# Attention stage of a four-layer kernel: the gates' running products are broadcast by DMA instead of by TensorE, the state is carried by a diagonal matmul, the LayerNorm sums are taken by ScalarE

## What is computed

```
q = elu(0.25 x Wq')+1 ; k = elu(x Wk')+1 ; v = x Wv' ; gate = sigmoid(x Wg' + bg)     (one gate per head and token)
S_t = gate_t * S_{t-1} + k_t (outer) v_t ;  y_t = q_t S_t                              (16x16 state per head and sequence)
x1 = layernorm(x + y Wo')
```

## Time and profile before

| | |
|---|---|
| median of three runs | 1479.38 us |
| the profiled execution, its own time | 1477.29 us |
| its span in the profile | 1475.2 us |
| mean granted TensorE clock | 0.972 of full speed |
| attention stage (to the first instruction of the routing stage) | 0 to 326.5 us |
| busy over the span | PE 92%, DVE 56%, ACT 36%, POOL 21% |

### The profile page before, as it was taken

The page is one execution under the profiler, slowest core; times in us unless marked ns, Lnnn a source line. Parts: engine busy times, 40 slices in busy tenths (PEclk is TensorE's granted clock), DMA queues, the critical chain, the costliest instruction groups (busy, mean ns, idle before and its releaser), DMA issues. The chain is left out here.

```text
span 1475.2 us, 21868 instructions
## 1 busy us (share of the span) xinstructions
PE 1355.2 (92%) x7418; PEld 863.6 (59%) x7419; DVE 829.0 (56%) x1676; ACT 536.6 (36%) x1104; POOL 303.8 (21%) x357
## 2 busy tenths in 40 slices
PE   7898888889999899999999996969999999899996
PEld 4566666565545566666666664435666554477774
DVE  5999999976543122222222221447778855676764
ACT  5445555432101122222222221133444532467675
POOL 2123333221663000000000001613220000134444
PEclk9999999999999999999999998889999999999998
DMA  5544554629221111111111112303110000000001
GB/s 188 194 151 174 177 170 165 208 75 361 86 86 43 29 43 46 46 43 46 46 43 46 46 43 71 100 17 112 31 29 1 1 1 11 1 1 15 29 15 58
DMA packets 68226, 112.39 MB, mean 76 GB/s; under 512 B 9008, under 2 KB 53936, under 8 KB 64048
## 3 DMA queue, kind: packets, MB, share of 16 engines
q1 hardware_dynamic: 61584, 94.49, 19.2%
q0 software_dynamic: 6144, 16.79, 3.6%
q10 hardware_dynamic: 416, 0.03, 0.0%
HBM read 79.70 MB, written 31.59 MB: 75 GB/s over the span
## 5 line engine op out<-in xcount | busy, mean ns | idle before, releaser
L1681 POOL DMA_INDIRECT m_got<-outs,slot x64 | 61.2, 956 | 574.7 <-POOLq L2063 458.1
L1086 DVE TENSOR_TENSOR ro_h<-ro_bB,ro_sl 128x512 f32<-128x512 f32 x71 | 49.1, 691 | 222.2 <-PE ro_bB L1035 222.2
L515 DVE TENSOR_TENSOR_SCAN a_dcy<-a_gbc,a_ident 128x2048 f32<-128x2048 f32 x32 | 144.7, 4522 | 11.4 <-DMA a_gbc<-gd 7.5
L2035 POOL TENSOR_TENSOR q_hr<-q_hf,q_hr 128x512 fp32r<-128x512 f32 x64 | 83.4, 1314 | 287.6 <-ACT q_hr L1876 287.6
L1030 PE MATMUL ro_bA<-Win,ro_xT 128*128 x284 | 136.4, 603 | 0.7 <-ACT ro_xT L1057 0.5
L1042 PE MATMUL ro_bO<-Wout,ro_hT 128*128 x568 | 134.3, 379 | 0.9 <-DVE ro_hT L1079 0.9
L1042 PEld LDWEIGHTS ro_bO<-Wout,ro_hT 128*128 128x128 f32 x568 | 107.8, 190 | 45.6 <-issue 34.6
L1035 PE MATMUL ro_bB<-Wsw,ro_xT 128*128 x284 | 134.4, 596 | 0.0
L1079 DVE COPY ro_hT<-ro_bH 128x512 f32<-128x512 f32 x71 | 49.1, 691 | 101.3 <-PE ro_bH L1015 101.3
L1066 ACT ACTIVATE ro_yo<-ro_bO 128x256 f32<-128x256 f32 x71 | 27.2, 383 | 204.9 <-PE ro_bO L1042 204.9
L1035 PEld LDWEIGHTS ro_bB<-Wsw,ro_xT 128*128 128x128 f32 x284 | 54.5, 192 | 69.0 <-issue 69.0
(11 more groups left out here) (271 smaller groups left out, 2534.4 us busy)
## 6 DMA issues: line engine op xcount, KB each, us to landing
a_gbc<-gd SPq DMA_DIRECT2D x32, 1024.0 KB, 4.7
rows<-a_zero SPq DMA_DIRECT2D x8, 1152.0 KB, 10.4
ro_xg<-rows SPq DMA_DIRECT2D x71, 128.0 KB, 2.0
outs<-ro_yo SPq DMA_DIRECT2D x71, 128.0 KB, 1.7
a_xt<-in_xTt SPq DMA_DIRECT2D x8, 512.0 KB, 3.8
X<-in_x SPq DMA_DIRECT2D x8, 512.0 KB, 5.7
Win<-in_w_in SPq DMA_DIRECT2D x8, 512.0 KB, 10.7
Wsw<-in_w_sw SPq DMA_DIRECT2D x8, 512.0 KB, 10.6
```

What stands on the lines that cost most here:

```text
L515: v.tensor_tensor_scan(dcy[:, :], gbc[j % 2][:, :], ident16[:, :], 0.0, ALU.mult, ALU.add).then_inc(d_done, 1)
L1681: pool.indirect_dma_start(out=got[q % 2][k][:, t, :], out_offset=None, in_=mem["outs"], in_offset=bass.IndirectOffsetOnAxis(ap=slot[:, k, ...
L2035: pool.tensor_tensor(hr[:, 1, f % 4, :], hf[f % 2][:, :], hr[:, 0, f % 4, :], ALU.subtract).then_inc(hl_done, 1)
```

## The change

The running products ET go to DRAM (tensor `ed`) with four DMAs a chunk, and come back by two DMAs a tile, each row repeated for the 16 channels of its head, into ebc (four buffers). decayed_q reads ebc in SBUF. The state update is a matmul of a diagonal matrix dg (made by ScalarE from the last column of ebc) with the old state, added in PSUM to k times v, and VectorE only masks the sum into St. The LayerNorm sums come from two ScalarE instructions with accumulated outputs, one step later (tile n-2), and normalize, turn_x and router come one step later too (one more step in the loop). TensorE and ScalarE take project(n+5) early in the step, except in every fourth (Q % 4 == 0). spread stands behind phi(4T+10). ET of chunk 0 is not computed. The diff, shortened:

```diff
@@ sync
-                sp.dma_start(rep[:, :, :, :], io["rep"]).then_inc(cst_in, 16)
+                sp.dma_start(eye32[:, :], io["eye32"]).then_inc(cst_in, 16)
+                def decays_out(T):
+                    sp.wait_ge(e_done, T)
+                    for b in range(B):
+                        sp.dma_start(mem["ed"][T, b], ET[T % 2][32 * b:32 * b + H, :]).then_inc(ed_out, 16)
+                def decays_in(j):
+                    T, b = divmod(j, 4)
+                    if b == 0:
+                        sp.wait_ge(ed_out, 64 * T)
+                    if j >= 8:
+                        sp.wait_ge(qe_done, j - 7)
+                        sp.wait_ge(dg_done, 2 * min(j - 7, KEPT - 4))
+                    for g in range(G):
+                        sp.dma_start(ebc[j % 4][:, g, :], mem["ed"][T, b, 8 * g:8 * g + 8, :].unsqueeze(1).to_broadcast([8, DH, P])).then_inc(eb_in[j % 4], 16)
                     if n % 4 == 0 and n // 4 + 1 < NC:
                         gates_out(n // 4 + 1)
+                        decays_out(n // 4 + 1)
                     if n + 2 < NT:
                         gates_in(n + 2)
+                    if 4 <= n + 2 < NT:
+                        decays_in(n + 2)
@@ tensor
-                def decays(j):
...
                 def update(j):
-                    if j >= 3:
-                        pe.wait_ge(dec_done, j - 2)
...
-                                           start=True, stop=True)
+                                           start=(g == 0), stop=(j < 4), skip_group_check=True)
+                    if j >= 4:
+                        pe.wait_ge(dg_done, 2 * (j - 3))
+                        pe.wait_ge(st_done, j - 3)
+                        for g in range(G):
+                            for r in range(4):
+                                mm = pe.matmul(bK[32 * r:32 * r + 32, 32 * g:32 * g + 32], dg[j % 2][32 * r:32 * r + 32, g, :],
+                                               St[32 * r:32 * r + 32, j % 4, g, :], start=False, stop=True, skip_group_check=True)
...
-                    if tile(n - 3):
-                        decays(n + 1)
+                    if Q < NT and Q % 4 > 0:
+                        project(Q)
                     if tile(n - 1):
                         project_out(n - 1)
...
-                    if Q < NT:
+                    if Q < NT and Q % 4 == 0:
                         project(Q)
                     if tile(n + 1):
                         values(n + 1)
-                    if carries(n - 6):
-                        turn_x(n - 6)
+                    if carries(n - 7):
+                        turn_x(n - 7)
@@ scalar
+                def decay_matrix(j):
+                    act.wait_ge(eb_in[j % 4], 32 * (j // 4))
+                    if j >= 6:
+                        act.wait_ge(u_ready, j - 1)
+                    for g in range(G):
+                        act.activation(dg[j % 2][:, g, :], eye32[:, :], ACT.Copy, scale=ebc[j % 4][:, g, P - 1:P]).then_inc(dg_done, 1)
+                def moments(j):
...
+                    act.activation(scrap[:, :], X[:, j, :], ACT.Copy, scale=-1.0 / D, accum_out=mv[T % 2][:, b, 0:1]).then_inc(bn_done, 1)
+                    act.wait_ge(bn_done, j + 1)
+                    act.activation(scrap[:, :], X[:, j, :], ACT.Square, bias=mv[T % 2][:, b, 0:1], accum_out=mv[T % 2][:, b, 1:2]).then_inc(ag_done, 1)
                     if tile(n + 2):
                         masked_q(n + 2)
+                    if 4 <= n < KEPT:
+                        decay_matrix(n)
+                    if Q < NT and Q % 4 > 0:
+                        project(Q)
...
+                    if carries(n - 7):
+                        keep_x(n - 7)
+                    if tile(n - 2):
+                        moments(n - 2)
                     if carries(n - 6):
-                        keep_x(n - 6)
-                    if carries(n - 5):
-                        normalize(n - 5)
+                        normalize(n - 6)
@@ vector
                 def gate_decay(T):
                     v.wait_ge(sig_done, T + 1)
-                    if T >= 3:
-                        v.wait_ge(er_ready, 4 * (T - 2))
-                    v.tensor_tensor_scan(ET[T % 2][:, :], gT[T % 2][:, :], zeros[:, :], 1.0, ALU.mult, ALU.add).then_inc(e_done, 1)
+                    if T >= 1:
+                        if T >= 3:
+                            v.wait_ge(ed_out, 64 * (T - 2))
+                        v.tensor_tensor_scan(ET[T % 2][:, :], gT[T % 2][:, :], zeros[:, :], 1.0, ALU.mult, ALU.add).then_inc(e_done, 1)
...
                 def decayed_q(j):
-                    v.wait_ge(er_ready, j - 3)
-                    v.wait_ge(o_ready, j - 1)
+                    v.wait_ge(eb_in[j % 4], 32 * (j // 4))
...
-                    v.tensor_tensor(qE[j % 2][:, :, :], bK[:, HALF:HALF + D].rearrange("p (g t) -> p g t", g=G),
-                                    qk[T % 2][:, 0, :, b * P:(b + 1) * P], ALU.mult).then_inc(qe_done, 1)
-                    v.wait_ge(st_done, 2 * min(j - 1, KEPT))
-                    v.tensor_copy(dec[j % 2][:, :], bK[:, HALF + P - 1:HALF + D:P]).then_inc(dec_done, 1)
+                    v.tensor_tensor(qE[j % 2][:, :, :], ebc[j % 4][:, :, :], qk[T % 2][:, 0, :, b * P:(b + 1) * P], ALU.mult).then_inc(qe_done, 1)
                 def update(j):
...
-                    v.tensor_tensor(um[:, :, :], bK[:, 0:64].rearrange("p (g c) -> p g c", g=G), blk[:, :, :], ALU.mult).then_inc(um_done, 1)
...
-                    for g in range(G):
-                        v.scalar_tensor_tensor(out=St[:, b, g, :], in0=St[:, b, g, :], scalar=dec[j % 2][:, g:g + 1], in1=um[:, g, :],
-                                               op0=ALU.mult, op1=ALU.add).then_inc(st_done, 1)
+                    v.tensor_tensor(St[:, b, :, :], bK[:, 0:64].rearrange("p (g c) -> p g c", g=G), blk[:, :, :], ALU.mult).then_inc(st_done, 1)
                 def residual(j):
...
-                    v.bn_stats(stat[:, :], X[:, j, :]).then_inc(bn_done, 1)
...
-                    v.bn_aggr(mv[T % 2][:, b, :], stat[:, :]).then_inc(ag_done, 1)
@@ gpsimd
-                    if Q % 4 == 1 and Q >= 9:
-                        spread((Q - 9) // 4)
+                    if Q % 4 == 2 and Q >= 10:
+                        spread((Q - 10) // 4)
```

More of the change, by code:

```diff
@@ L107, in build_attention @@
         qE = [sb(f"qE{p}", [P, G, P]) for p in range(2)]
-        dec = [sb(f"dec{p}", [P, G]) for p in range(2)]
-        um = sb("um", [P, G, 32])
+        ebc = [sb(f"ebc{p}", [P, G, P]) for p in range(4)]
+        eye32, dg = sb("eye32", [P, 32]), [sb(f"dg{p}", [P, G, 32]) for p in range(2)]
         St = sb("St", [P, B, G, 32])
         yT = [sb(f"yT{p}", [P, G, P]) for p in range(2)]
-        stat = sb("stat", [P, 6])
+        scrap = sb("scrap", [P, D])
         mv = mem["mv"]
-        nmean = sb("nmean", [P, B])
         shift = [sb(f"shift{p}", [P, B]) for p in range(2)]
@@ L154, in state_read @@
         def state_read(e, j):
[L156 to L159, removed]
+            e.wait_ge(st_done, j + 1)
         with nc.Block() as block:
@@ L420, in values @@
                     act.wait_ge(v_ready, j + 1)
-                    if tile(j - 7):
-                        act.wait_ge(xnt_ready, j - 6)
+                    if tile(j - 8):
+                        act.wait_ge(xnt_ready, j - 7)
                     if j >= 2:
@@ L445, in score @@
                     act.activation(mem["score"][:, j, :], bY[:, R0:R0 + E8], ACT.Copy).then_inc(r_read, 1)
+                def moments(j):
+                    T, b = divmod(j, 4)
+                    act.wait_ge(res_done, j + 1)
+                    if T >= 2 and b == 0:
+                        act.wait_ge(sh_done, T - 1)
+                    if j >= 1:
+                        act.wait_ge(ag_done, j)
+                    act.activation(scrap[:, :], X[:, j, :], ACT.Copy, scale=-1.0 / D, accum_out=mv[T % 2][:, b, 0:1]).then_inc(bn_done, 1)
+                    act.wait_ge(bn_done, j + 1)
+                    act.activation(scrap[:, :], X[:, j, :], ACT.Square, bias=mv[T % 2][:, b, 0:1], accum_out=mv[T % 2][:, b, 1:2]).then_inc(ag_done, 1)
                 def normalize(j):
@@ L624, in spread @@
                     y = rstd[T % 2][:, :]
-                    link(pool.tensor_scalar(nt[:, :], mv[T % 2][:, :, 1], 1.0, EPS, ALU.mult, ALU.add))
+                    link(pool.tensor_scalar(nt[:, :], mv[T % 2][:, :, 1], 1.0 / D, EPS, ALU.mult, ALU.add))
                     link(pool.tensor_scalar(y.bitcast(I32), nt[:, :].bitcast(I32), -0.5, float(0x5F3759DF), ALU.mult, ALU.add))
@@ L637, in _ @@
                     phi(Q)
-                    if Q % 4 == 1 and Q >= 9:
-                        spread((Q - 9) // 4)
-                for T in range((NT - 1 - 9) // 4 + 1, NC - 1):
+                    if Q % 4 == 2 and Q >= 10:
+                        spread((Q - 10) // 4)
+                for T in range((NT - 1 - 10) // 4 + 1, NC - 1):
                     spread(T)
```

(9 more changed lines are left out.)

75 lines of the change are left out of this document (23 added, 52 removed).

## The result

| | before | changed |
|---|---|---|
| median | 1479.01 us (1476.52 to 1483.12, 4 runs) | 1512.78 us (1512.04 to 1515.41, 4 runs) |
| profiled execution: own time, span | 1477.29, 1475.2 | 1515.41, 1513.6 |
| attention stage ends at | 326.5 | 362.7 |
| mean granted clock | 0.972 | 0.952 |

The ratio is 1.0223 [1.0202, 1.0243]: slower, by 33.8 us. The prediction was 1465 and faster. The stage accounts for it: it ends 36.2 us later, and what follows it takes 1151.0 instead of 1148.7.

A forecast was written before the change was run, and what follows sets the result against it. VectorE was taken as the bound, 38.89 of 40 us busy. Six cycles -8.4, start -1.5, steps 0 to 3 -3.5, tail 0, late spread -0.3, together -13.7, gave 1465; range 1446 to 1477.

The forecast's parts named there:

- GpSimd, the heart of it: Prediction's step on GpSimd and VectorE shutting each other out over SBUF: decayed_q hit, spread late, cycle 37.1 us, 1.4 less.
- C: Fourth step of VectorE's four-step cycle; phi is behind spread, only a 0.2 us instruction gets ahead of decayed_q: 0.2.
- G: Gates step, first of VectorE's four-step cycle, 10.44 us before; projection late, phi holds the next scan by 0.36.
- Rival 1: decayed_q isn't hit by phi: cycle about 35.4 us, time 1456, with the floor of 33.0 1441; chance 0.27.
- Rival 2: GpSimd eats the rest, all hits and latest spread: cycle 37.9 us or as before, 1475, no change; chance 0.20.
- Rival 3: Diagonal matmuls run one by one in TensorE's update: 3.2 us, cycle 43.2, time 1503, slower; chance 0.08.
- Decayed_q is hit: VectorE's decayed_q, now reading SBUF, stands while phi goes first on GpSimd: 1.2 us each in two steps of four.
- A: Second step of VectorE's four-step cycle, 9.13 us before; phi was to make decayed_q stand for 1.2 us.
- B: Third step of VectorE's four-step cycle; phi at +4.5, scan end +4.98 from scores, so decayed_q stands for 1.2 us.
- VectorE's floor: VectorE's step without the dropped instructions: 9.13 less 1.02 becomes 8.11 us, floor of the four-step cycle 33.0.
- diagonal matmuls: 16 instructions added to update on TensorE: taken as 0.3 us, bounds 0.3 and 3.2.
- The tail: Last five steps: lose about 3, the added step costs 1.3, two tail steps with moments 0.8 each: 0.

The follow-up runs named there:

- e8: Changed kernel with ScalarE's two sums moved two places up, ahead of values and keep_x: 1465.86 us, ratio 0.9903 to the kernel before.
- e5: Changed kernel with 15 extra matmuls of zeros on TensorE while scores wait for phi: 1481.64 us, ratio 1.0129 to the kernel before.
- e1: Changed kernel with two Newton steps in spread instead of three, four instructions fewer: 1455.45 us, ratio 0.9944 to the kernel before.
- e4: Changed kernel with all projections back behind attend, spread left in its place: 1495.93 us, ratio 1.0222 to the kernel before.
- e7: Changed kernel with ScalarE's sums early, all projections behind attend and spread behind phi(4T+9): 1440.56 us, ratio 0.985 to the kernel before.
- e2: Changed kernel with the LayerNorm sums back on VectorE and spread back behind phi(4T+9): 1469.0 us, ratio 1.0035 to the kernel before.
- e9: Changed kernel with sums back on VectorE, spread behind phi(4T+9) and all projections behind attend: 1454.7 us, ratio 0.9945 to the kernel before.

## Why the prediction was wrong

**The step that failed** is the placing of spread in "GpSimd, the heart of it": "it starts about when C does: three of its 14 instructions get in before the scan, eleven after it ... so phi(4T+3) begins 8.2 after C begins and ends 1.2 into G". The runs showed in its place that no instruction gets in before the scan, that G's scan holds the chain once more with phi behind it, and that TensorE waits 7 us for phi and not 1.2. Four things are wrong in it.

- *The start.* It lies 0.5 us behind the scan's, not ahead of it. No instruction got in; the first was held 3.90. The start was a sum of ScalarE's whole step, told to "about". e8 shows that 1.8 us decide.
- *The count.* There are 15 instructions, not 14 (and 16 before, where the text ahead of the prediction says 15).
- *The door of G.* The sum had the rule that a scan shuts GpSimd out, used it for C, and never asked where G's scan stands. By its own numbers C begins with the scores, its scan ends at 4.98, and G's scan starts at 8.31 + 0.56 = 8.9. Phi at 8.2 was 0.7 us ahead of a door of 4.4, a margin of two or three instructions that the text doesn't name. With no instruction in before the scan, and one more in the chain, there is nothing left of it.
- *The clock.* A wait of TensorE was priced at its own length. One of 7 us costs 1.5 to 4.5 more, 2.9 in the mean, by e5. The earlier trace rows has 1.00, and no row there gives this price; it belonged in the range as an unknown of the wait.

Rival 1 had the true start in a half-sentence: "spread starts 1.2 into C, has all its instructions behind the scan" (measured: 1.37 behind the scores of C). It then let phi end 2 into G. By its own numbers phi would begin at 4.98 + 14 x 0.28 = 8.9, where G's scan stands (8.7 with its C of 8.11): the shut door was in the text, unread, beside the price of the fastest case. Rival 2 had the right place ("GpSimd is in order and spread's place is later") with the wrong price, 1475. Its 37.9 us a cycle grew smoothly with spread's lateness, where e1 shows a jump: 1.1 us of GpSimd work made 7.8 us a cycle in the mean. Rival 3, the only slow case, was a different mechanism, and false. So the chance of slower, 0.08, was too small, and 1512.78 is 36 us above the range.

**What held.** The start: 1.5 us sooner. *Decayed_q is hit* in A, 1.42 for 0.40, a price of 1.0 against the 1.2 taken. In B it is not hit at all, and there rival 1 was right: phi came at scores + 4.78 for the predicted 4.5 and the scan ended at + 4.87 for 4.98, so that 0.1 was left of the margin of 0.5. That B is 10.01 in some cycles, near the predicted 9.3, is luck: it is the clock. The rule of the Trainium skill (SBUF — State Buffer, Who interferes with whom) that old decayed_q was safe and the new one isn't agrees with 0.40 and 1.42; who goes next when both wait came from the rows. *VectorE's floor* of 8.11 a step: e4 has 8.01 in A and C, and e7 8.17. The *diagonal matmuls*: 0.26 against 0.3, rival 3's 3.2 did not come. *The sums*: from the first sum's start to normalize it is 1.1 us against 1.2; dg 0.3 each, overlapping. *The DMA part*: taken as 0, and between 60 and 300 us no scan waits for gbc.

On the sums, the Trainium skill (ScalarE: Activation LUTs, Rules for kernel authors) would have them stay on VectorE. Its price of 1.0 us, an estimate, is close to the 1.1 measured. Its advice fits the change as made (e2, sums on VectorE, 1.0035 against 1.0223) and not the better orders: with late projections, sums on ScalarE give 0.985 (e7) and on VectorE 0.9945 (e9). There VectorE is the bound and ScalarE, at 28.5 of 40 busy, is not.

**The tail** was taken as 0. Behind the last scan it is +4.3, with 1.5 won in the two steps ahead of it: some +2.8 in the prediction's terms. The last steps have no scan and no projection, so ScalarE's chain of sums and normalize is the path. TensorE's wait for it in the timeline of the changed kernel (L293 is turn_x, L299 the router):

```profile
355.00 0.44 PE L293 MATMUL a_bV<-ident,X 128*128 128x128 f32 x2 [0.62 <-ACT X L470]
356.00 0.58 PE L299 MATMUL a_bY<-a_Wr,XT 128*128 128x8 f32 x4 [0.57 <-ACT XT L450]
357.43 0.44 PE L293 MATMUL a_bV<-ident,X 128*128 128x128 f32 x2 [0.84 <-ACT X L470]
```

2.43 us a step, where the prediction had one step of 1.3 and two times 0.8.

The account of the stage by the prediction's terms: start -1.5; all other steps, A, B and C above all, -14.3; the long steps +47.6, of which 17.1 are clock by e5; behind the last scan +4.3; 36.1 in the sum.

## What to carry to other kernels

When a chain of small dependent instructions on GpSimd shares SBUF with long two-input instructions of VectorE, its cost is not its length but how many of the long ones it meets: list the gaps (here 3.5 us between scans of 4.4), see where the chain starts in them, whether it and its reader start inside, and who waits for that reader, and treat a margin of tenths of a microsecond as a coin toss with the whole long instruction as the stake. When a producer moves to another engine, place the release of its readers before counting what the move saves; here the same sums earlier in ScalarE's order turned 2.2% slower into 1.4% faster. And price a long idle of TensorE with the slower matmuls that follow it.

## What the runs showed of the hardware that was not expected

- A one-input tensor_scalar on GpSimd (128x4) is shut out by the scan as well: 3.90 us instead of 0.19, ending with the scan.
- Who goes next is decided by tenths of a microsecond: with phi 0.45 us ahead of the scan's end decayed_q takes 1.42 (A), with phi 0.1 ahead of it 0.40 and phi is the one held, 1.55 for 1.27 (B).
- The exclusion goes both ways with scans: with phi in its way (e1) a scan lasts 4.99, and in e9 5.46, instead of 4.42.
- A ScalarE instruction with an accumulated output is followed by a second row, ACTIVATION_READ_ACCUMULATOR, of 0.18 to 0.26 us, most of it beside the next one: two sums of 128x256 cost 1.1 us from start to start.
- After 7 us of idle TensorE's next groups run at the lower clock (scores 2.09 for 1.15), for 2.5 to 10 us; matmuls of zeros in the idle time keep it up (e5). In two of the five B steps from 100 us on the clock also fell behind a wait of 1.25 and 1.30 us; in the other three, behind 1.30 and 1.31 us, it did not.
